# Decayed keys turned by DMA transposes from the second 512 tokens on, and the first early x tiles requested behind the output projection

## The chip, the cores and the metric

The kernel runs on the 8 cores of one Trainium2 chip. Each core takes two of the 16 sequences and works alone; no core sends data to another. The metric is the device time of the slowest core, in microseconds (us). Three executions of the kernel before gave a median of 3469.9 us (3467.58 to 3722.14).

## What is computed

One layer, on x of 16 sequences x 2048 tokens x 2048 features:

```
x = x + 0.5 * ffn(layernorm(x))
x = x + attn(layernorm(x))
x = x + 0.5 * ffn(layernorm(x))
```

ffn rounds its input row by row to 8-bit integers and its weight to -1, 0 or 1, multiplies them (2048 x 2048) and scales back. attn is gated linear attention with 16 heads of 128 features: q, k, v and a gate g (log-sigmoid) are projections of x; per head a 128x128 state follows S = S * exp(g) + k v^T and y = q S, token by token. The y of all heads is normalised and multiplied by the output weight Wo.

## The kernel before

**Tiling.** A core has 4096 tokens, in 8 slabs (g = 0 to 7) of 512 tokens; a slab is 4 tiles (t) of 128 tokens. TensorE goes through phases, each over one slab: P1 is the first ffn, H is the gate, key and query projections of 16 heads with the attention behind them, V is the values, P4 the output projection, P5 the second ffn (P6 is a last piece of it). The order is V(0), then for each g: H(g), P1(g+1), P4(g), V(g+1), P5(g). The phases P1, V, P4 and P5 consist of 16 groups (k) of 16 matmuls of 512 columns, written by `fat` (L511). A head of H has three groups of 16 matmuls (L597).

**Weights.** They pass through a ring of three SBUF buffers, one *unit* at a time: a head's 1.5 MB or a quarter of a 2 MB-unit matrix. The list `units` fixes the order. In slab 0 (and for heads 3, 7, 11 and 15 in slab 1) POOL reads the fp32 weight by a casting DMA (L446), and SP then writes the bf16 result to a scratch tensor in HBM (L412); afterwards SP reads from that scratch (L409). A load of unit n waits until TensorE is through with unit n - 3.

**A head.** ACT and DVE make decay factors from the gate. DVE writes the scaled keys kt, then the decayed keys kd (L795, two buffers, kd[h % 2]), then the scaled queries. `post(g, h)` runs on TensorE after the second projection group of head h + 1: four transposes of kd into PSUM (L546), then eight small matmuls for the scores (L554, L556). ACT copies the transposed keys to SBUF, into kdT (L1032). `step(g, hg, t)` runs after all three groups of a head, from head 4 on, and uses four heads' kdT (L571) and scores (L581, L584); a group of four heads is first used one head after its last one, and the last group in P1(g+1).

**SP's program.** SP works down one list: for each unit n it loads (or writes to scratch) unit n, and then runs what belongs to unit n - 3, called `done`: stores of the output, or the *crossings* (L370). A crossing is a DMA transpose of one normalised token tile nb, 128 x 2048 of 2 bytes, into the operand xT. Crossings for A (the next slab's P1) come behind heads 6 to 9. Everything on SP is in order: an instruction that waits holds back all behind it.

**Early x.** For g of 2 and more POOL asks for slab g's four x tiles ahead of time, cast to bf16, into qp and kdT (L463), once step(g - 2, 3, 3) is done; the buffers are idle then. DVE reads them in `ahead(g)`, behind quantise("C", g - 2) and before its first evacuation of P5(g - 2): 4 moments, a maximum and a minimum per tile. The same x is later loaded again into its residual buffer (L425), behind P5(g - 2).

Of the kernel before, what the change touches and what calls it, by code (L numbers as in the profile page):

```python
# [17 lines left out]
H = 16  # L18
SEQ = 2
L = 2048  # L20
TPS = 4
# [29 lines left out]
def emit(SEQ, L, known):  # L51
# [108 lines left out]
    with contextlib.ExitStack() as ctx:  # L160
# [27 lines left out]
        kdT = sb("kdT", 8 * 512, BF16, 2)  # L188
# [78 lines left out]

        XT = [count(f"turned{t}") for t in range(TPS)]

        def xTof(g):  # L270
            return xT[(g + 1) % 2]

# [47 lines left out]
        def crossed(kind, g):  # L320

            return (kind in "AL" and g >= 2) or (kind == "C" and g < NSL - 1)


        nb_sets = [("A", 0), ("L", 0)]
        for g in range(NSL):
# [28 lines left out]
        def _(e):  # L355
# [11 lines left out]
            def cross(kind, g, t):  # L367
# [3 lines left out]
                                      [:, :, t * 128:(t + 1) * 128], in_=nbt(t)  # L371
                                      ).then_inc(*XT[t].up(kind, g, by=16))

            def crossings(done):

                (kind, g), b = done
                if kind == "H" and crossed("A", g + 1) and 6 <= b <= 9 and g + 1 < NSL:
                    cross("A", g + 1, b - 6)
                if kind == "P1" and crossed("L", g) and b == 3:
                    cross("L", g, 0)  # L380
                if kind == "P4" and crossed("L", g + 1) and g + 1 < NSL and b == 0:
                    cross("L", g + 1, 1)
                if kind == "P4" and crossed("L", g + 1) and g + 1 < NSL and b == 1:
                    cross("L", g + 1, 2)
                    cross("L", g + 1, 3)
                if kind == "P4" and crossed("C", g) and b == 3:
                    cross("C", g, 0)
                if kind == "V" and g > 0 and b == 0:
                    cross("C", g - 1, 1)
                if kind == "V" and g > 0 and b == 1:  # L390
                    cross("C", g - 1, 2)
                    cross("C", g - 1, 3)

            for n in range(NU + 3):
                done = units[n - 3] if n >= 3 else (("none", 0), 0)
                if done[0][0] in ("P5", "P6"):
                    for t in range(3):
                        store(done, t)
                if n < NU:
                    (kind, g), b = units[n]  # L400
                    cols = NB * (384 if kind == "H" else 512)
                    scratch = PLAIN[kind][1] if kind in PLAIN else s_f
                    if not is_cast(n) and not is_kept(n):
                        before, kept = ring_before(n), kept_at(n)
                        e.wait_ge(*TD.of("unit", before))
                        if is_kept(before):
                            e.wait_ge(*WB[place(before)].of(before))
                        e.wait_ge(*WB[place(kept)].of(kept))
                        e.dma_start(out=buf(n)[:, 0:cols], in_=scratch[b]).then_inc(*RL[place(n)].up(n, by=16))  # L409
                    elif is_kept(n):  # L410
                        e.wait_ge(*(VD.of("tern", n, 3) if kind == "P1" else RC[place(n)].of(n)))
                        e.dma_start(out=scratch[b], in_=buf(n)[:, 0:cols]).then_inc(*WB[place(n)].up(n, by=16))  # L412
                if done[0][0] in ("P5", "P6"):
                    store(done, 3)
                else:
                    crossings(done)
# [5 lines left out]
        def _(e):  # L422
# [36 lines left out]
            for g in range(2, NSL + 1):  # L459
                if g < NSL:  # L460
                    e.wait_ge(*TD.of("Y", g - 2, 3, 3))
                    for t in range(TPS):
                        e.dma_start(out=xe(t), in_=xrows[g * TPS + t]).then_inc(*XE[t].up(g, by=16))  # L463
                    e.wait_ge(*VD.of("ev", ("P5", g - 2), 15))
                    load_x(g)
# [7 lines left out]
        def _(e):  # L473
            ti = 0
# [65 lines left out]

            def post(g, h):
                nonlocal ti
                e.wait_ge(*VD.of("kd", g, h))
                e.wait_ge(*SD.of("pT", ti - 2))
                for t in range(TPS):
                    tr = e.transpose(pT[ti % 2][:, t * 128:(t + 1) * 128],  # L546
                                     kd[h % 2][:, t * 128:(t + 1) * 128], ident[:])
                tr.then_inc(*TD.up("kdT", g, h))
                ti += 1
                e.wait_ge(*VD.of("qo", g, h))  # L550
                if g or h:
                    e.wait_ge(*(VD.of("Asb", g, h - 1) if h else VD.of("Asb", g - 1, H - 1)))
# [8 lines left out]
            def step(g, hg, t):  # L561
                now = S[(g * TPS + t) % 2]
                if t == 0:
                    e.wait_ge(*SD.of("kdT", g, 4 * hg + 3))
                    e.wait_ge(*VD.of("Asb", g, 4 * hg + 3))
                before = step_before(g, hg, t)
                if before is not None:
# [88 lines left out]
        def _(e):  # L656
# [132 lines left out]
            def decayed_keys(g, h):  # L789
                k2 = kt[h % 2][:].rearrange("p (t a c) -> p t a c", a=4, c=64)[:, :, 0:4:3, :]  # L790
                e.wait_ge(*SD.of("smx", g, h))
                e.wait_ge(*VD.of("ev", ("H", g), 3 * h + 1))
                f8 = smx[:, h * 20 + 4:h * 20 + 12].rearrange("p (t a) -> p t a", a=2) \
                    .unsqueeze(3).broadcast_to([128, TPS, 2, 64])
                e.tensor_tensor(kd[h % 2][:].rearrange("p (t a c) -> p t a c", a=2, c=64), k2, f8, ALU.mult  # L795
# [203 lines left out]
        def _(e):  # L999
# [41 lines left out]
            def heads(g):  # L1041
                for h in range(H):
# [13 lines left out]
                        e.wait_ge(*VD.of("cleared"))  # L1056
                    if g == 0 and h == 11:
                        e.wait_ge(*WB[3].of(aside[0]))
                    if h > 0:
                        keys_turned(g, h - 1)  # L1060
                    if h >= 4:
                        y_out(g, h // 4 - 1, h % 4)
# [4 lines left out]
                            turned("A", g + 1, i)  # L1067

            def tail(g, k):
                if k == 1:  # L1070
                    keys_turned(g, H - 1)
                if 2 <= k <= 5:
                    y_out(g, 3, k - 2)
# [125 lines left out]
```

## Time and profile before

| | |
|---|---|
| median of 3 executions | 3469.9 us |
| profiled execution, device time | 3467.16 us |
| its span, first to last instruction of core 7, the slowest | 3465.6 us |
| spans of cores 0 to 7 | 3457.2, 3444.7, 3453.1, 3458.6, 3454.9, 3440.9, 3464.2, 3465.6 us |
| mean granted TensorE clock of the cores | 0.990 to 0.992 |
| TensorE matmuls (PE) | 3321.8 us busy, 96% of the span |
| DVE, ACT | 2018.9 us (58%), 744.6 us (21%) |
| DMA queue of SP, of POOL | 49.3% and 14.6% of the 16 DMA engines' span |

A timeline row gives start, duration (us), engine, line, operation, tiles written and read, shapes and count; idle time before it and what ended that stand in brackets. Matmuls overlap, so what one costs is the distance between starts. SPq is SP's sequencer while it issues a DMA; the duration there is how long SP was held. "DMA to landing" is the time from issue to completion. A row of `stretches` gives the stretch, its length, the busy time and number of instructions of PE, PEld (weight loads), DVE, ACT and POOL, and then the granted TensorE clock, the share of DMA time and GB/s. All rows are of core 7 where no other is named.

### The profile page before, as it was taken

What the parts mean: (1) busy time and instruction counts of PE and PEld (TensorE: products, weight loads), DVE (VectorE), ACT (ScalarE), POOL (GpSimd) and SP (SyncE); (2) the same over time, 40 slices, a digit from 0 to 9 for tenths busy, and PEclk for the clock granted to TensorE, in tenths of its full rate; (3) what the DMA queues carried; (4) which work ended last, traced back from release to release, by engine and by line L of the source; (5) the groups of instructions that cost most, each with busy time, mean ns of one, the idle gap of its engine ahead of it and who ended that gap; (6) DMA issues with size and microseconds to landing.
All of it is one profiled execution on the core that took longest, in us unless ns stands there. A gap on an engine that the chain in (4) does not pass through costs nothing.

```text
span 3465.6 us, 49427 instructions; the slowest of 8 cores (3440.9 to 3465.6 us)
## 1 busy us (share of the span) xinstructions
PE 3321.8 (96%) x18210; PEld 1611.7 (47%) x18210; DVE 2018.9 (58%) x3783; ACT 744.6 (21%) x1297; POOL 48.3 (1%) x94
## 2 busy tenths in 40 slices
PE   1789998999999999999999999999999999999999
PEld 0334453445544454445544455444554455444544
DVE  5626767156672666637664476826667366635663
ACT  5312321023200221113211232002320032112210
POOL 0000000000000000000000000000000000000000
PEclk9899999999999999999999999999999999999999
DMA  7899979787566546665466655666556654553453
GB/s 221 193 225 204 219 179 231 202 199 195 177 194 200 170 159 183 191 198 170 150 188 204 177 169 171 182 200 172 176 168 197 202 157 161 163 170 145 153 176 134
DMA packets 227642, 634.68 MB, mean 183 GB/s; under 512 B 165856, under 2 KB 165888, under 8 KB 189520
## 3 DMA queue, kind: packets, MB, share of 16 engines
q1 hardware_dynamic: 215104, 553.68, 49.3%
q0 software_dynamic: 12304, 77.85, 14.6%
q8 instruction: 151, 2.47, 0.3%
q14 instruction: 83, 0.68, 0.1%
HBM read 585.35 MB, written 83.89 MB: 193 GB/s over the span
## 4 chain that ended last, share of the span: by engine, by line
PE 87%; DMA 9%; DVE 1%; issue 1%; another core or an unknown queue 1%; SPq 0%; ACT 0%; DVEq 0%; POOLq 0%; ACTq 0%; POOL 0%
PE pj L511 47%; PE pj L597 35%; DMA ring<-wh 2%; DMA s_v<-first 1%; DMA ring<-wv 1%; DMA s_h<-ring 1%; DMA fw<-fw 1%; PE pT L488 1%; DMA ring<-wo 1%; PE pP L571 1%; PE pY L581 1%; PE pT L546 1%; PE pA L554 1%; PE pY L584 1%
## 5 line engine op out<-in xcount | busy, mean ns | idle before, releaser
L511 PE MATMUL pj<-ring,xT 128*128 128x512 bf16 x8000 | 1755.4, 380 | 31.5 <-DVE bnA L722 12.4
L597 PE MATMUL pj<-xT,ring 128*128 128x512 bf16 x6144 | 1369.3, 380 | 28.2 <-DMA ring<-wh 23.6
L511 PEld LDWEIGHTS pj<-ring,xT 128*128 128x128 f16 (+1 forms) x8000 | 779.1, 98 | 955.0 <-issue 45.1
L597 PEld LDWEIGHTS pj<-xT,ring 128*128 128x128 bf16 x6144 | 590.4, 98 | 711.5 <-issue 40.8
L765 DVE TENSOR_TENSOR_SCAN Cs<-rest_s,lsg 128x512 f32<-128x512 bf16 x128 | 156.6, 1223 | 301.8 <-ACT lsg L1049 300.6
L962 DVE SCALAR_TENSOR_TENSOR ost<-pj,coC,res 128x512 f32<-128x512 f32 x112 | 84.1, 751 | 405.5 <-PE pj L511 405.5
L1046 ACT ACTIVATE lsg<-pj 128x512 f32<-128x512 f32 x128 | 76.4, 597 | 736.4 <-PE pj L597 729.6
L759 DVE SCALAR_TENSOR_TENSOR res<-pj,coA,res 128x512 bf16<-128x512 f32 x128 | 95.7, 748 | 174.4 <-PE pj L511 174.4
L804 DVE TENSOR_TENSOR qt<-pj,E 128x512 bf16<-128x512 f32 x128 | 88.4, 691 | 133.1 <-PE pj L597 133.1
L1039 ACT CAST vy<-pY 128x512 bf16<-128x512 f32 x128 | 75.0, 586 | 369.5 <-PE pY L584 349.4
L1083 ACT CAST vy<-pj 128x512 bf16<-128x512 f32 x128 | 74.9, 585 | 366.9 <-PE pj L511 366.9
L1051 ACT ACTIVATE E<-Dl 128x512 bf16<-128x512 f32 x128 | 80.6, 630 | 301.0 <-DVE sm L774 293.5
L833 DVE SCALAR_TENSOR_TENSOR S<-S,smx,pP 128x128 bf16<-128x128 bf16 x480 | 134.6, 342 | 12.8 <-DVE qp L812 0.5
L759 DVE SCALAR_TENSOR_TENSOR res<-pj,res 128x512 bf16<-128x512 f32 x128 | 88.2, 689 | 89.8 <-PE pj L511 89.8
L785 DVE TENSOR_TENSOR kt<-pj,E 128x512 bf16<-128x512 f32 x128 | 88.5, 692 | 77.3 <-ACT smx L1053 76.7
L1023 ACT ACTIVATE xT<-pT,bet,gam 128x512 bf16<-128x512 bf16 x128 | 92.2, 775 | 161.4 <-PE pT L488 161.4
L771 DVE TENSOR_TENSOR Dl<-Cs 128x512 f32<-128x512 f32 x128 | 88.6, 692 | 13.7 <-DVE Cs L765 0.5
L812 DVE TENSOR_TENSOR qp<-qt,smx 128x512 bf16<-128x512 bf16 x128 | 88.6, 692 | 13.7 <-DVE qt L808 0.5
L722 DVE BATCH_NORM_STATS2 bnC<-res 128x6 f32<-128x512 bf16 x128 | 88.8, 694 | 13.2
L1049 ACT ACTIVATE lsg<-lsg,one 128x512 f32<-128x512 f32 x128 | 92.5, 723 | 12.2 <-ACT lsg L1046 0.4
L722 DVE BATCH_NORM_STATS2 bnL<-res 128x6 f32<-128x512 bf16 x128 | 88.1, 689 | 9.2 <-DVE res L759 0.5
L1005 ACT ACTIVATE lnvC<-mvC,eps 128x4 f32<-128x4 f32 x8 | 2.4, 298 | 403.2 <-DVE mn4C L672 403.2
(121 smaller groups left out, 2187.1 us busy)
## 6 DMA issues: line engine op xcount, KB each, us to landing
ring<-s_h SPq DMA_DIRECT2D x108, 1536.0 KB, 8.2
ring<-s_f SPq DMA_DIRECT2D x60, 2048.0 KB, 9.3
ring<-s_v SPq DMA_DIRECT2D x28, 2048.0 KB, 9.9
ring<-s_o SPq DMA_DIRECT2D x28, 2048.0 KB, 9.8
out<-ost SPq DMA_DIRECT2D x128, 256.0 KB, 4.3
ring<-wh POOLq DMA_DIRECT2D x20, 1536.0 KB, 21.7
s_h<-ring SPq DMA_DIRECT2D x16, 1536.0 KB, 20.2
fw<-fw SPq DMA_DIRECT2D x16, 1024.0 KB, 35.9
```

Source lines behind the costliest of these rows:

```text
L511: return e.matmul(bank(phase, k)[:], xt[:, ic * SLAB + t * 128:ic * SLAB + (t + 1) * 128], buf(n)[:, ic * 512:(ic + 1) * 512], start=ic == ...
L597: mm = e.matmul(bank(phase, 3 * h + j)[:], buf(n)[:, ic * 384 + j * 128:ic * 384 + (j + 1) * 128], xt[:, ic * SLAB:(ic + 1) * SLAB], start ...
L722: e.bn_stats(bn[kind][:, (t * 4 + b) * 6:(t * 4 + b + 1) * 6], src[:, b * 512:(b + 1) * 512]).then_inc(*VD.up())
L759: e.scalar_tensor_tensor(x, bank(phase, k)[:], combo(t), x, ALU.mult, ALU.add).then_inc(*VD.up("ev", phase, k))
L765: e.tensor_tensor_scan(Cs[:], rest[:], lsg[:], 0.0, ALU.mult, ALU.add).then_inc(*VD.up())
L771: e.tensor_tensor(Dl[:].rearrange("p (n c) -> p n c", c=64), c64, c64[:, :, 31:32].broadcast_to([128, 8, 64]), ALU.subtract).then_inc(*VD. ...
L785: e.tensor_tensor(k2, p[:].rearrange("p (t a c) -> p t a c", a=2, c=64), E2[:].rearrange("p (t a c) -> p t a c", a=2, c=64), ALU.mult).the ...
L804: e.tensor_tensor(q3[:, :, 0:3:2, :], p[:].rearrange("p (t a c) -> p t a c", a=2, c=64), E1[:].rearrange("p (t a c) -> p t a c", a=2, c=64 ...
L812: e.tensor_tensor(qp[:, (h % 8) * 512:(h % 8 + 1) * 512].rearrange("p (t c) -> p t c", c=128), q192[:, :, 0:128], smx[:, h * 20:h * 20 + 4 ...
L833: e.scalar_tensor_tensor(nxt[:, hs], now[:, hs], smx[:, h * 20 + 16 + t:h * 20 + 17 + t], pP[:, i * 128:(i + 1) * 128], ALU.mult, ALU.add) ...
L1023: e.activation(dst[:, ic * 512:(ic + 1) * 512], pT[ti % 2][:, j * 512:(j + 1) * 512], ACTF.Identity, bias=bet[:, ic:ic + 1], scale=gam[:, ...
L1049: e.activation(lsg[:], lsg[:], ACTF.Ln, bias=one1[:]).then_inc(*SD.up("l", g, h))
```

## The change

Two things. From slab 1 on (`keys_crossed(g)`, g > 0), the four TensorE transposes of a head and ACT's copy are gone, and SP issues a DMA transpose of kd[h % 2] (128 x 512, 2 bytes) straight into kdT. It stands ahead of the load of the unit in turn. `step` waits for the two DMA counters in place of ACT's, and DVE's kd of head h waits for the crossing of head h - 2. And POOL waits, for g == 2 alone, until the last group of P4(0) before it asks for the early x tiles.

```
+        KX = [count(f"keys_turned{i}") for i in range(2)]
...
+        def keys_crossed(g):
+            return g > 0
...
+            def cross_keys(g, h):
+                e.wait_ge(*VD.of("kd", g, h))
+                e.wait_ge(*(TD.of("kv", g, h // 4 - 2, 3) if h >= 8 else TD.of("kv", g - 1, h // 4 + 2, 3)))
+                e.dma_start_transpose(out=kdT[:, (h % 8) * 512:(h % 8 + 1) * 512].rearrange("p (t c) -> p t c", c=128),
+                                      in_=kd[h % 2][:]).then_inc(*KX[h % 2].up(g, h, by=16))
...
                 if done[0][0] in ("P5", "P6"):
                     for t in range(3):
                         store(done, t)
+                if done[0][0] == "H" and keys_crossed(done[0][1]):
+                    cross_keys(done[0][1], done[1])
                 if n < NU:
...
                 if g < NSL:
                     e.wait_ge(*TD.of("Y", g - 2, 3, 3))
+                    if g == 2:
+                        e.wait_ge(*TD.of("fat", ("P4", 0), 15))
                     for t in range(TPS):
                         e.dma_start(out=xe(t), in_=xrows[g * TPS + t]).then_inc(*XE[t].up(g, by=16))
...
             def post(g, h):
...
-                e.wait_ge(*VD.of("kd", g, h))
-                e.wait_ge(*SD.of("pT", ti - 2))
-                for t in range(TPS):
-                    tr = e.transpose(pT[ti % 2][:, t * 128:(t + 1) * 128],
-                                     kd[h % 2][:, t * 128:(t + 1) * 128], ident[:])
-                tr.then_inc(*TD.up("kdT", g, h))
-                ti += 1
+                if not keys_crossed(g):
+                    e.wait_ge(*VD.of("kd", g, h))
+                    e.wait_ge(*SD.of("pT", ti - 2))
+                    for t in range(TPS):
+                        tr = e.transpose(pT[ti % 2][:, t * 128:(t + 1) * 128],
+                                         kd[h % 2][:, t * 128:(t + 1) * 128], ident[:])
+                    tr.then_inc(*TD.up("kdT", g, h))
+                    ti += 1
...
             def step(g, hg, t):
                 if t == 0:
-                    e.wait_ge(*SD.of("kdT", g, 4 * hg + 3))
+                    if keys_crossed(g):
+                        e.wait_ge(*KX[0].of(g, 4 * hg + 2))
+                        e.wait_ge(*KX[1].of(g, 4 * hg + 3))
+                    else:
+                        e.wait_ge(*SD.of("kdT", g, 4 * hg + 3))
...
             def decayed_keys(g, h):
+                if keys_crossed(g) and h >= 2:
+                    e.wait_ge(*KX[h % 2].of(g, h - 2))
...
-                    if h > 0:
+                    if h > 0 and not keys_crossed(g):
                         keys_turned(g, h - 1)
...
-                if k == 1:
+                if k == 1 and not keys_crossed(g):
                     keys_turned(g, H - 1)
```

## Rows read from the trace of the kernel before

**Rows 1.** The page: chain of waits, shares of the span by engine.

```profile
PE 87%; DMA 9%; DVE 1%; issue 1%; another core or an unknown queue 1%; SPq 0%; ACT 0%; DVEq 0%; POOLq 0%; ACTq 0%; POOL 0%
```

**Rows 2.** PE's waits, 400 to 700 us, then 700 us on: total, times, longest.

```profile
PE pj L511 <- DVE bnA L722: 12.4, 1, 12.4
PE pj L511 <- DMA ring<-wo: 1.7, 1, 1.7
...
PE pj L597 <- DMA ring<-s_h: 2.9, 1, 2.9
```

**Rows 3.** Timeline of PE, one head of slab 2.

```profile
1154.86 0.39 PE L546 MATMUL pT<-ident_s,kd 128*128 128x128 bf16 x4
1155.08 0.22 PE L554 MATMUL pA<-qt,kt 128*128 128x128 bf16 x1
...
1166.45 0.39 PE L546 MATMUL pT<-ident_s,kd 128*128 128x128 bf16 x4
```

**Rows 4.** Slab 0: landing of the first two wo casts, the last, then two s_v loads.

```profile
DMA to landing us min/median/max: 14.3/18.3/22.4
...
DMA to landing us min/median/max: 31.0/31.0/31.0
...
DMA to landing us min/median/max: 26.7/29.7/32.8
```

**Rows 5.** Timelines of PE and SP, slab 0's end: V(1) starts; its first loads.

```profile
576.37 112.38 PE L511 MATMUL pj<-ring,xT 128*128 128x512 bf16 x512 [12.43 <-DVE bnA L722]
...
549.32 16.86 SPq L409 DMA_DIRECT2D ring<-s_v  x3
```

**Rows 6.** Stretches: end of slab 0, then the heads of slab 2.

```profile
517.00:549.00 32.00, 30.41 (x177) 15.12 (x175) 22.34 (x35) 6.07 (x6) 2.64 (x5) 1.00 1.00 223
564.00:577.00 13.00, 0.63 (x2) 0.28 (x3) 11.68 (x31) 0.50 (x2) 0.00 (x0) 0.59 1.00 254
577.00:600.00 23.00, 23.00 (x101) 10.12 (x100) 23.00 (x21) 3.52 (x6) 0.00 (x0) 0.94 0.91 260
1105.00:1290.00 185.00, 185.00 (x1106) 92.91 (x1105) 120.47 (x259) 55.36 (x107) 2.12 (x4) 1.00 0.56 169
```

**Rows 7.** Early x tiles 3 and 4, issued at 519 us, then at 1313 us.

```profile
DMA to landing us min/median/max: 54.7/59.3/63.8
...
DMA to landing us min/median/max: 20.6/21.5/22.4
```

**Rows 8.** Timeline of DVE: first and last pass over early x, first P5 evacuation.

```profile
575.51 2.46 DVE L722 BATCH_NORM_STATS2 bnA<-qp 128x6 f32<-128x512 bf16 x4
...
600.36 2.27 DVE L740 TENSOR_REDUCE mnbA<-kdT 128x4 f32<-128x2048 bf16 x1
637.07 0.75 DVE L962 SCALAR_TENSOR_TENSOR ost<-pj,coC,res 128x512 f32<-128x512 f32 x1 [34.44 <-PE pj L511]
```

**Rows 9.** Line 370, all crossings: duration in ns, landing; then one issued alone.

```profile
L370 SPq DMA_TRANSPOSE xT<-nb x76: 1747/7822/15689, 573.9 to 3080.0; - x76
DMA to landing us min/median/max: 4.3/10.2/17.8
...
L370 SPq DMA_TRANSPOSE xT<-nb x1: 1747/1747/1747, 3054.0 to 3054.0; - x1
```

**Rows 10.** Timelines, slab 2: DVE's kd of one head; SP at the end of its projections.

```profile
1180.54 0.69 DVE L795 TENSOR_TENSOR kd<-kt,smx 128x512 bf16<-128x512 bf16 x1
...
1182.70 0.32 SPq L409 DMA_DIRECT2D ring<-s_h  x1
1183.14 7.80 SPq L370 DMA_TRANSPOSE xT<-nb  x1
```

**Rows 11.** Timeline of SP, slab 1: the scratch write of head 3.

```profile
722.03 0.33 SPq L412 DMA_DIRECT2D s_h<-ring  x1
```

**Rows 12.** Line 412: the landing of that write.

```profile
DMA to landing us min/median/max: 7.7/7.7/7.7
```

**Rows 13.** Timeline of PE, core 3: the start of V(1).

```profile
570.17 1.44 PE L511 MATMUL pj<-ring,xT 128*128 128x512 bf16 x3 [7.00 <-DMA ring<-s_v]
```

## The prediction

> **What bounds the kernel.** I read four views. The chain of waits comes first: 87% of it is TensorE and 9% DMA [rows 1]. So time taken out of TensorE's own stream counts one for one, nearly everywhere, and the DMAs count only where TensorE stands. The list of PE's waits says where that is: from 400 to 700 us two waits belong together, 1.7 us for the last wo cast and 12.4 us before V(1), and after 700 us the largest single wait is 2.9 us for a weight load [rows 2]. The 12.4 us are put down to DVE's pass over early x, but that pass starts at 575.51 us [rows 8] and gives V(1) nothing it needs. What ends then is a load: V(1)'s first unit was asked for at 549.32 us [rows 5], the two loads of that moment took 26.7 and 32.8 us to land [rows 4], and 549.3 + 26.7 = 576.0 us, just before V(1) starts at 576.37 us [rows 5]. The stretches give the reason: the DMA share is 1.00 from 517 to 549 us and from 564 to 577 us [rows 6]. In the heads of slab 2 TensorE is busy for all of 185 us at a DMA share of 0.56 [rows 6]. There it is TensorE alone that sets the pace.
>
> **Part 1, the transposes leave TensorE.** In a head the first transpose starts at 1154.86 us and the first score matmul behind the four at 1155.08 us: 0.22 us, with no wait between [rows 3]. The change takes this from 16 heads in each of 7 slabs, 112 in all: 112 x 0.22 = **24.6 us**. Rounding in the row leaves 23.5 to 25.8 us. ACT loses 112 copies, which I cost at nothing since ACT is not on the path; the scores and the mask on DVE come as before.
>
> **What comes for it: SP and the DMA queue.** The crossing of a head is a quarter of those that the kernel has. The trace has no crossing of this size, so I bound it. Of 76 large ones, the shortest hold of SP is 1.75 us and the shortest landing 4.3 us; that hold belongs to one issued with nothing ahead of it [rows 9]. The median is 7.8 us and 10.2 us [rows 9], for crossings issued 0.44 us behind a weight load, as in [rows 10]. So a key crossing holds SP between 0.44 us (a quarter of 1.75) and 7.8 us, and lands within 2 to 10 us. I take about 1 us and 4 us in an ordinary head, since it is issued into an empty queue: kd is complete at 1180.54 + 0.69 = 1181.23 us, and SP only asks for the next unit at 1182.70 us, when the head's projections are over [rows 10]. SP therefore sees kd 1.5 us before it would have been released anyway, and the load behind it moves by nothing or by tenths. The key DMA finds the previous load landed, a period of 11.59 us (1166.45 - 1154.86, [rows 3]) being longer than its flight. Who waits for it: `step` needs head 4hg + 3 one whole head later, 11.4 us against a landing of 4; DVE's kd of head h needs the crossing of h - 2, two heads later, 22 us. Behind head 15, two groups of P1 and a score block lie between. Cost on the path: 0.
>
> In heads 6 to 9 of a slab SP also issues a crossing for A, 7.8 us of hold [rows 10]. A period then holds 1 + 0.3 + 7.8 us and two gaps of 0.4, about 10 of the 11.4 us that a head takes after the change. It fits, with little left over.
>
> **Where it does cost: slab 1.** Heads 3, 7, 11 and 15 are still cast there, and SP is stuck until the cast has landed. It writes head 3 to scratch at 722.03 us [rows 11], and then today asks at once for head 4, for which TensorE already waits 2.9 us [rows 2]. Now head 1's key crossing goes between, behind a write that takes 7.7 us to land [rows 12]. Head 4's load is late by at least 0.4 us (the hold) and at most by the 7.7 us in which the write drains. I take **+2 us**: the engines are never idle meanwhile, so the queue only has the crossing's own data more to move. Heads 7, 11 and 15 have the same order, but their next load isn't waited for today.
>
> **Part 2, early x goes later.** The four tiles are asked for at 518 to 520 us, among the last cast, two scratch writes and V(1)'s loads. The first wo casts landed in 14.3 and 22.4 us, the last, issued just ahead of the x tiles, in 31.0 [rows 4]. SP can't ask for V(1) until it has landed. With x out of the way it should land in about 23 us, V(1)'s load goes out 8 us sooner, and has less beside it. The last two x tiles took 54.7 and 63.8 us, so nearly all four tiles moved before 576 us [rows 7]. Their work in a less loaded place is bounded by the 20.6 to 22.4 us that the same tiles need in slab 1 [rows 7], with a load beside them; I put it at 13 us of all engines. A saturated queue gives that back as it is. The two waits are 14.1 us [rows 2]; and the granted clock is 0.59 (of 2.4 GHz, so partly at 1.2) in the idle stretch and still 0.94 in the 23 us behind it [rows 6], so ending the stall returns up to 23 x 0.06 = 1.4 us more. I take **13 us**, between 0 and 15.5.
>
> The x tiles now start at 562.3 us, when P4(0) ends. DVE's pass takes 27.1 us (575.51 to 600.36 + 2.27, [rows 8]), 6.8 a tile, and must be over when the first group of P5(0) is, 60.7 us after V(1)'s start [rows 5, 8], so at about 623 us. The last tile has to land by 616 us, 54 us after the request. I expect 25 to 40 us: the DMA share from 577 to 600 us was 0.91 with the old x tiles in it [rows 6]. Cost 0.
>
> **Sum.** 3467.16 - 24.6 - 13 + 2 = **3431.6 us** against the profiled execution. The median of three is 2.7 us above that execution, so a median should lie between 3431.6 and 3434.3: I say 3433, which is -1.1%. Core 3, with a span of 3458.6 us and a wait of 7.0 us in place of 12.4 [rows 13], comes out at 3458.6 - 24.6 - 7 + 2 = 3429, so core 7 or 6 stays last.
>
> **Rivals.**
> - *x moved for nothing.* The queue was full before x was asked for (the second cast took 22.4 us [rows 4]), and scratch writes keep it full. V(1) still starts late: 3467 - 24.6 + 2 = 3445. Against it: core 3's wait is only 7.0 us [rows 13], so the load is near its need. 12%.
> - *x too late.* If the last tile takes 63.8 us again [rows 7], it lands at 626, DVE ends at 633 and P5(0) stands 10 us: 3442. The queue is emptier there. 6%.
> - *Small crossings disturb the loads.* 112 x 512 packets more, and a load or two late at each slab's start, where SP's queue also holds stores: 1.5 to 3 us a slab, 3442 to 3453. The share of 0.56 speaks against it. 8%.
> - *SP saturated: slower.* The place is heads 7 to 10 of slabs 1 to 6, where key crossing, load and crossing for A share SP. If a key crossing holds SP 7.8 us like a large one, a head takes 7.8 + 0.3 + 7.8 + 0.8 = 16.7 us of SP's 11.4; the lag is 5.3 a head, 21 us after four. Head 11's crossing starts that late and lands 10 us on, and the step behind head 12 stands about 21 + 10 - 12.5 = 18 us. Six slabs make 110 us: 3467 - 38 + 2 + 110 = 3541, slower by 2.1%. It decides from a hold of 2.5 us (lag begins), and is a net loss from about 4.6. For it: 7.8 is the median. Against: kd comes into an empty queue, where a crossing four times the size held 1.75 us. 6%, with half of it above 2%.
>
> The Trainium skill (VectorE: DVE Perf Modes, "The three transpose paths") prices a 128x128 bf16 transpose at 390 ns on TensorE and 1309 ns by the DMA crossbar, and its rules say to use TensorE where the result may go to PSUM. By its figures part 1 would return 448 x 0.39 = 175 us, where the rows show 0.055 us a transpose behind other work, and a key crossing would take 5.2 us, an estimate from that page that lies beyond the 4.6 of the last rival. The rule speaks against this change; the trace has 16 blocks landing in 4.3 us [rows 9], 0.27 each, and I follow the trace.
>
> **Chances and range.** The forecast (3426 to 3440) has 68%, the rivals 12, 6, 8 and 6. The range of 3423 to 3455 takes in all but the last, with the other bounds of the terms. 2% either way (69 us) is about what a measurement of this kernel can tell from no change. Faster by over 2% would need twice the gain: 2%. Slower by over 2%: 4%. Within 2%: 94%.
>
> **What would show it.** Right: a head's period of 11.37 us in place of 11.59; SP holds at keys of 1 us or so, landings under 5; V(1) starting by 565 us; head 4 of slab 1 waiting 3 to 6 us; early x landed by 602 us. Wrong: PE waiting at L571 for DMA, SP's loads sliding after head 10, DVE waiting before L795, or P5(0) waiting for a bank that DVE empties late.

## The result, and the profile after

| | before | changed |
|---|---|---|
| median of all executions | 3596.02 us (4) | 3433.89 us (4) |
| range | 3467.58 to 4092.39 | 3430.6 to 3650.42 |
| profiled execution | 3467.16 | 3432.75 |
| spans of the cores | 3440.9 to 3465.6 | 3415.1 to 3431.2 |

The ratio is 0.9889, with a 95% interval of 0.985 to 0.9927: about 1.1% faster, and clear of 1. It leaves out executions in which the cores of one half of the chip got a lower clock; two of the four before were such, which is why that median is so high. The point forecast was 3433.

The page of the changed kernel: its span and instruction count, the busy line, SP's DMA queue and the chain's shares.

```profile
span 3431.2 us, 48546 instructions; the slowest of 8 cores (3415.1 to 3431.2 us)
...
PE 3299.2 (96%) x17762; PEld 1588.8 (46%) x17762; DVE 2019.6 (59%) x3783; ACT 691.1 (20%) x1185; POOL 49.8 (1%) x94
...
q1 hardware_dynamic: 276032, 568.38, 53.5%
...
PE 89%; DMA 8%; DVE 1%; issue 1%; SPq 0%; ACT 0%; DVEq 0%; POOLq 0%; ACTq 0%; POOL 0%
```

TensorE has 448 matmuls fewer, ACT 112 copies fewer, and its share of the chain is 89%, where it was 87% [rows 1]: the bound has not moved. SP's queue is busier by 4 points of the DMA engines' time.

Line numbers have shifted: L546 is L565 and serves slab 0 alone, L554 is now L573, L597 is L620, L511 is L529, L409 is L424, L412 is L427, L370 is L376, L571 is L594, L795 is L820; the key crossing is L384.

**Part 1.** PE's timeline in slab 2, the first score matmul of two heads in a row, answers to [rows 3].

```profile
1152.45 0.22 PE L573 MATMUL pA<-qt,kt 128*128 128x128 bf16 x1
...
1163.82 0.22 PE L573 MATMUL pA<-qt,kt 128*128 128x128 bf16 x1
```

The distance is 11.37 us, where it was 11.59. The key crossing (L384) and the crossings of normalised tokens (L376), durations in ns and landings in us, answer to [rows 9]; SP's timeline around the end of a head answers to [rows 10].

```profile
L384 SPq DMA_TRANSPOSE kdT<-kd x112: 1172/1175/2713, 690.7 to 3245.8; - x112
...
DMA to landing us min/median/max: 2.4/2.4/21.9
```

```profile
L376 SPq DMA_TRANSPOSE xT<-nb x76: 1746/7750/11481, 580.5 to 3048.3; - x76
DMA to landing us min/median/max: 4.3/9.9/17.2
```

```profile
1167.34 1.18 SPq L384 DMA_TRANSPOSE kdT<-kd  x1
1168.67 0.46 SPq L424 DMA_DIRECT2D ring<-s_h  x1
1169.23 8.24 SPq L376 DMA_TRANSPOSE xT<-nb  x1
1178.50 1.17 SPq L384 DMA_TRANSPOSE kdT<-kd  x1
```

and DVE's kd of the second of these heads:

```profile
1177.68 0.68 DVE L820 TENSOR_TENSOR kd<-kt,smx 128x512 bf16<-128x512 bf16 x1
```

A key crossing holds SP 1.18 us and lands in 2.4 (median). Key crossing, load and crossing of x fill 10.1 us (1167.34 to 1169.23 + 8.24), and the next key crossing goes out 11.2 us after the first: SP is nearly full here, but it waits for the keys and not the keys for it. It is free at 1177.47 us, kd is complete at 1178.36, and the crossing goes out at 1178.50.

**Part 2.** The waits of PE from 400 to 700 us, then the longest from 700 us on, answer to [rows 2].

```profile
PE pj L620 <- DMA ring<-wh: 2.3, 1, 2.3
PE pP L594 <- DVE Asb L844: 2.0, 1, 2.0
...
PE pj L620 <- DMA ring<-s_h: 2.4, 1, 2.4
```

Both waits, for the last wo cast and before V(1), are gone. The landings of the last wo cast, of V(1)'s first two loads, and of early x tiles 3 and 4 answer to [rows 4, 7]; SP's first load of V(1) to [rows 5].

```profile
DMA to landing us min/median/max: 27.9/27.9/27.9
...
DMA to landing us min/median/max: 14.1/17.5/21.0
...
DMA to landing us min/median/max: 19.7/20.9/22.0
```

```profile
554.69 16.40 SPq L424 DMA_DIRECT2D ring<-s_v  x3
```

V(1)'s first load landed at 554.69 + 14.1 = 568.8 us. POOL asked for x at 571.1 us, once the last group of P4(0) was over, so the load had some 2 us to spare on this core. Between the request of the last wo cast and this landing lie 42.6 us (526.2 to 568.8), where they were 58.3 (517.7 to 576.0).

The stretches around it answer to [rows 6] (length, busy time and count of PE, PEld, DVE, ACT and POOL, granted clock, DMA share, GB/s):

```profile
526.00:554.00 28.00, 28.00 (x162) 13.91 (x160) 19.88 (x32) 5.06 (x5) 0.53 (x1) 1.00 0.99 234
554.00:571.00 17.00, 17.00 (x98) 8.46 (x97) 10.87 (x18) 3.04 (x3) 0.00 (x0) 1.00 0.95 309
571.00:594.00 23.00, 23.00 (x109) 10.43 (x107) 18.18 (x37) 3.91 (x8) 2.11 (x4) 1.00 1.02 238
594.00:631.00 37.00, 37.00 (x173) 16.78 (x172) 19.70 (x17) 5.86 (x10) 0.00 (x0) 1.00 0.93 256
1092.00:1271.00 179.00, 179.00 (x1034) 88.33 (x1033) 118.08 (x252) 47.87 (x92) 2.12 (x4) 1.00 0.69 183
```

The engines are no less full than before; the full stretch has moved behind the first load of V(1), where TensorE does not need them, and the granted clock is 1.00 in all of it. DVE's timeline shows the price (answers to [rows 8]): a wait of 3.5 us for x, and 16.5 us left over before P5(0) where it had 34.4.

```profile
585.82 2.47 DVE L745 BATCH_NORM_STATS2 bnA<-qp 128x6 f32<-128x512 bf16 x4 [3.54 <-DMA qp<-x]
...
629.42 0.75 DVE L987 SCALAR_TENSOR_TENSOR ost<-pj,coC,res 128x512 f32<-128x512 f32 x1 [16.48 <-PE pj L529]
```

**Where the time went, by stage.** I measured these from the starts of the first projection matmul of a slab's heads and of the first group of the phase behind them, on all eight cores of one profiled execution each. H is a slab's heads; F0 reaches from the end of slab 0's heads to the start of slab 1's. Mean of the cores, and their range:

```
                     H(0)                F0                  H(1)                H(2)     F1
before               216.4 (211-220)     243.2 (239.7-247.3) 184.6 (182.2-188.4) 182.3    227.8
changed              220.8 (215-227)     231.1 (231.0-231.2) 180.9 (179.2-183.2) 178.9    227.6
keys alone           218.4 (212-223)     243.4 (239.9-245.4) 180.2 (178.9-183.5) 178.9    227.6
later x alone        218.9 (213-223)     231.9 (231.0-234.7) 183.7 (182.5-185.9) 182.3    227.8
changed, again       219.0 (215-223)     231.7 (231.0-234.0) 182.0 (179.9-185.5) 178.9    227.6
keys not turned      218.0 (215-221)     231.1 (231.0-231.2) 179.4 (178.9-179.9) 178.9    227.6
x behind cast        214.8 (209-223)     232.3 (231.0-233.9) 184.8 (181.2-187.7) 179.4    227.8
later x, all slabs   215.3 (212-222)     231.1 (231.0-231.2) 180.4 (178.9-182.1) 179.3    227.6
```

(In the rows "x behind cast" and "later x, all slabs", pairs of cores took 0.7 to 1.8 us more in most of the slabs from 2 on; the mean granted clock of these cores was 0.986 to 0.991, of the others 0.990 to 0.993.) Each later slab gains 3.3 us in its heads and 0.2 in the phase behind them: 16 x 0.22.

### The profile page after: what moved, and what is told of

Its sections match the earlier page's. It is cut to its first block, busy times and chain, and to the rows that moved or that the text cites. A ratio compares the mean times of both kernels' runs of the same rounds, so it can differ in the third digit from the quotient of the medians.

```text
span 3431.2 us, 48546 instructions; the slowest of 8 cores (3415.1 to 3431.2 us)
## 1 busy us (share of the span) xinstructions
PE 3299.2 (96%) x17762; PEld 1588.8 (46%) x17762; DVE 2019.6 (59%) x3783; ACT 691.1 (20%) x1185; POOL 49.8 (1%) x94
## 4 chain that ended last, share of the span: by engine, by line
PE 89%; DMA 8%; DVE 1%; issue 1%; SPq 0%; ACT 0%; DVEq 0%; POOLq 0%; ACTq 0%; POOL 0%
PE pj L529 50%; PE pj L620 34%; DMA ring<-wh 4%; DMA ring<-wv 1%; DMA fw<-fw 1%; PE pT L506 1%; DMA s_h<-ring 1%; PE pP L594 1%; PE pY L604 1%; PE pA L573 1%; PE pY L607 1%; SPq L365 0%; DVE ring L774 0%; PE pA L575 0%; DMA ring<-s_h 0%
## 5 line engine op out<-in xcount | busy, mean ns | idle before, releaser
L529 PE MATMUL pj<-ring,xT 128*128 128x512 bf16 x8000 | 1753.0, 380 | 16.8 <-DVE ring L774 9.6
L620 PE MATMUL pj<-xT,ring 128*128 128x512 bf16 x6144 | 1372.6, 381 | 29.9 <-DMA ring<-wh 23.0
L529 PEld LDWEIGHTS pj<-ring,xT 128*128 128x128 f16 (+1 forms) x8000 | 778.8, 98 | 938.1 <-issue 26.7
L620 PEld LDWEIGHTS pj<-xT,ring 128*128 128x128 bf16 x6144 | 591.4, 98 | 715.5 <-issue 46.9
L745 DVE BATCH_NORM_STATS2 bnC<-res 128x6 f32<-128x512 bf16 x128 | 88.8, 694 | 13.9 <-DVE res L782 0.9
L820 DVE TENSOR_TENSOR kd<-kt,smx 128x512 bf16<-128x512 bf16 x128 | 87.7, 685 | 2.1 <-DMA kdT<-kd 1.3
```

Source lines behind the costliest of these rows:

```text
L529: return e.matmul(bank(phase, k)[:], xt[:, ic * SLAB + t * 128:ic * SLAB + (t + 1) * 128], buf(n)[:, ic * 512:(ic + 1) * 512], start=ic == ...
L620: mm = e.matmul(bank(phase, 3 * h + j)[:], buf(n)[:, ic * 384 + j * 128:ic * 384 + (j + 1) * 128], xt[:, ic * SLAB:(ic + 1) * SLAB], start ...
L745: e.bn_stats(bn[kind][:, (t * 4 + b) * 6:(t * 4 + b + 1) * 6], src[:, b * 512:(b + 1) * 512]).then_inc(*VD.up())
```

## The experiments

**Keys alone.** The changed kernel without the wait before the early x requests.

```
-                    if g == 2:
-                        e.wait_ge(*TD.of("fat", ("P4", 0), 15))
```

> The key crossings alone; early x is asked for where the kernel before asks. My theory, that the two parts are independent and add: 16 heads x 0.22 us in each of seven slabs, 24.6 us, so 3443 to 3446 us, a ratio near 0.9929; each later slab's stretch from its first head projection to P1 falls from 182.2 to 178.9 us; V(1) still stands 7 to 12 us. The rival, that most of the gain hangs on the x requests (a fuller queue makes the key crossings late while x is in flight), says 3455 us or more.

Measured: 3440.6 to 3445.59 us, median 3443.5, ratio 0.9927 (0.9908 to 0.9946). V(1) stands 11.0 us for its load on the slowest core, and the F0 column is that of before. The term of 24.6 us holds, and the rival (3455 us or more) falls. The wait, on core 0 of this kernel:

```profile
PE pj L526 <- DMA ring<-s_v: 11.0, 1, 11.0
```

**Later x alone.**

```
         def keys_crossed(g):
-            return g > 0
+            return False
```

> The later x requests alone; all keys are turned on TensorE. My theory: the stall before V(1) goes, so the stretch from P1(1) to the first head of slab 1 falls from 240 to 247 us to about 231.5 us on every core, and the slowest core gains 13 to 16 us if the heads of slab 0 take the same: 3453 to 3456 us, ratio 0.996. The rival, that what is saved there comes back as longer loads in slab 0's heads or in slab 1 (those heads were 7.2 us longer on core 7 in the one profile of the changed kernel, before any changed instruction), says 3462 us or more, with slab 0's heads at 222 us or more on most cores.

Measured: 3449.88 to 3453.95 us, median 3452.56, 0.9952 (0.9933 to 0.9971). F0 falls to 231 to 234.7 us. The rival asked for slab 0's heads at 222 us or more on most cores; one core has that (223.1), and their mean is 218.9: the time didn't come back. By the medians beside them (before 3466.6 in seven executions, changed 3429.9 in four), the parts are worth 23 and 14 us, and together 37.

**The changed kernel again.** No edit.

> The changed kernel once more, to see its spread and slab 0's heads in another execution. If the 4 us by which slab 0's heads were longer on the mean of the cores are chance, they lie near 216 to 219 us here on the mean, and the time is 3428 to 3434 us. If they belong to the change, they are again 220 us or more on the mean. Sum of the parts: the gain of this one equals those of the two single edits, 24.6 + 14, within 3 us.

Measured: 3425.94 to 3432.99 us, 0.9884 (0.9858 to 0.9911). Slab 0's heads come to 219.0 on the mean. That lies at the border of the two branches of the expectation. But the code of that stage is unchanged in all eight rows of the table, and its mean runs from 214.8 to 220.8. So the longer heads of slab 0 in the first profile of the changed kernel (220.8) are within the spread of this stage, in which TensorE waits for casts (23.0 us in six waits on core 7 of the changed kernel). The gain is that of the two parts.

**Keys not turned.** From slab 1 on, no transpose by either engine, and nothing waits for one, DVE's kd included. The kernel leaves the turned keys out, so its output isn't that of the layer; only its time is of use.

```
-                if done[0][0] == "H" and keys_crossed(done[0][1]):
-                    cross_keys(done[0][1], done[1])
...
-                    if keys_crossed(g):
-                        e.wait_ge(*KX[0].of(g, 4 * hg + 2))
-                        e.wait_ge(*KX[1].of(g, 4 * hg + 3))
-                    else:
+                    if not keys_crossed(g):
                         e.wait_ge(*SD.of("kdT", g, 4 * hg + 3))
```

> From slab 1 on the keys are not turned at all: neither by TensorE nor by DMA, and nothing waits for it, so the state update there uses old data. Everything else as in the changed kernel. This takes away all that the key crossings cost. My theory says that they cost nothing on the path from slab 2 on and at most 2 us in slab 1: 3429 to 3433 us, the changed kernel minus 0 to 2. The rival, that 57344 further packets slow the loads here and there, says 5 us or more below the changed kernel.

Measured: 3423.43 to 3424.38 us, against 3425.94 to 3432.99 beside it: 6 us by the medians, more than I expected (0 to 2). The place is as expected: from slab 2 on the stretches are equal to 0.1 us, and slab 1's heads fall from 182.0 (worst core 185.5) to 179.4 (worst 179.9). The other two profiled executions of the changed kernel have 180.9 (183.2) and 181.3 (184.5), so the crossings cost 1.5 to 2.6 us there on the mean of the cores and 3.3 to 5.6 between the worst ones, by one execution without them. The rival named the size, my theory the place. Core 4 of the changed kernel, again, and of this one, PE's waits in slab 1:

```profile
PE pj L620 <- DMA ring<-s_h: 3.0, 1, 3.0
PE pj L620 <- DMA ring<-wh: 1.6, 1, 1.6
```

```profile
PE pj L615 <- DMA ring<-s_h: 0.9, 1, 0.9
```

**Each key crossing seven times.** This tests the prediction's slower rival: six more crossings of kd into idle staging space, in slabs 1 to 6. The edit also has DVE wait for them before it writes kd again, and its output evacuations before they use the space.

```
...
+                    for d in dumps:
+                        e.dma_start_transpose(out=d.rearrange("p (t c) -> p t c", c=128),
+                                              in_=kd[h % 2][:]).then_inc(*KD.up(g, h, by=16))
```

> In slabs 1 to 6 SP issues each key crossing seven times, once into kdT and six times into a part of the output staging buffer that is idle then; kd is only rewritten when all seven have landed. One crossing holds SP 1.17 us, so seven hold it 8.2 us: this sets up the state of the prediction's slower rival, a hold of 7.8 us a head. My theory, that SP's hold counts only where it exceeds a head's 11.4 us: SP needs 8.2 + 0.5 + 8.2 us plus gaps in heads 7 to 10, lags 5 to 6 us a head, and by head 12 TensorE stands at the step or at a weight load for 10 to 20 us a slab: 60 to 120 us in six slabs, 3490 to 3550 us, with the stalls on the waits for the crossings or the loads in heads 11 to 13 and none before head 8. The opposing theory, that the queue's data is what counts: 7 x 57344 packets spread evenly, a few tenths of a us on every head from head 1 on, and under 30 us in all.

Measured: 3687.7 us, 1.0646 (1.0628 to 1.0664), 254 us above the changed kernel; I expected 60 to 120. The heads of slabs 2 to 6 take 207 to 211 us on the mean of the cores, some 30 more each, and those of slab 1 245 us (up to 262), some 64 more. SP's timeline, core 0, slab 2, one late head:

```profile
1279.59 1.19 SPq L386 DMA_TRANSPOSE kdT<-kd  x1
1280.87 9.05 SPq L395 DMA_TRANSPOSE ost<-kd  x6
1290.08 0.47 SPq L435 DMA_DIRECT2D ring<-s_h  x1
1290.64 6.46 SPq L378 DMA_TRANSPOSE xT<-nb  x1
```

and what TensorE waits for there:

```profile
1279.84 9.58 PE L631 MATMUL pj<-xT,ring 128*128 128x512 bf16 x32 [5.04 <-DMA ring<-s_h]
1297.45 8.75 PE L631 MATMUL pj<-xT,ring 128*128 128x512 bf16 x32 [3.56 <-DMA ring<-s_h]
1314.53 0.58 PE L605 MATMUL pP<-vy,kdT 128*128 128x128 bf16 x4 [4.54 <-DMA kdT<-kd]
```

The seven hold SP 10.2 us and not 8.2; that the later ones are held by the data queued ahead is my reading. So SP has no reserve even in heads 0 to 6, and waits of 0.4 to 1.8 us stand there too, before the stalls of 3.6 to 5.0 us. The mechanism of the rival exists, at the step's wait for the crossing and at the loads; a hold of 1.18 us is far from it. The price per slab (30 us, 64 in slab 1) is more than the rival's 18. The run can't part SP's hold from the data of six more crossings, which come with it.

**Key crossing behind the load.**

```
                 if done[0][0] in ("P5", "P6"):
                     for t in range(3):
                         store(done, t)
-                if done[0][0] == "H" and keys_crossed(done[0][1]):
-                    cross_keys(done[0][1], done[1])
...
+                if done[0][0] == "H" and keys_crossed(done[0][1]):
+                    cross_keys(done[0][1], done[1])
                 if done[0][0] in ("P5", "P6"):
                     store(done, 3)
```

> Each key crossing stands behind the load of the unit in turn in place of ahead of it (and ahead of the crossing for A). My theory of the two kinds of hold, that SP is held by the data queued ahead: the hold goes from 1.2 us to 5 us or more and the landing from 2.4 to 8 to 10 us. The step needs it within 11 us, so slabs 2 to 7 lose 0 to 3 us each, mostly at heads 8 and 12, and the load of head 4 in slab 1 leaves at once, which returns up to 2 us there: 3430 to 3450 us. The rival, that the hold is a matter of the crossing's own descriptors and not of what is ahead, says hold 1.2 us, landing up to 10 us, and the changed kernel's time within 2 us.

Measured: 3441.16 and 3436.14 us, too few for an interval. The mean granted clock in the profiled one was 0.985 to 0.990 on cores 4 to 7 and 0.991 to 0.993 on cores 0 to 3, so I read the latter. Core 0:

```profile
L384 SPq DMA_TRANSPOSE kdT<-kd x112: 1195/1710/3110, 695.1 to 3226.5; - x112
...
DMA to landing us min/median/max: 5.8/7.4/15.6
```

The hold is 1.7 us and not 5; the landing goes from 2.4 to 7.4 us. My theory of the hold fails for a crossing this small: a load ahead delays its landing and hardly holds SP. Slabs 2 to 7 take 178.2 to 178.9 us on these cores, as in the changed kernel, and slab 1's heads 179.8 to 180.6, so 7.4 us still fits in the 11.4 that the step leaves. Whether this order is as good as the changed kernel's, two executions don't tell.

**Slab 0 too.**

```
         def keys_crossed(g):
-            return g > 0
+            return True
```

> The keys are turned by DMA in slab 0 too. There SP stands at each scratch write until the cast has landed, so a head's crossing leaves two heads late. My theory: TensorE saves 16 x 0.22 = 3.5 us and loses it again at the four steps' first use, where the crossing of head 4hg + 3 waits behind the cast of head 4hg + 5; each of four steps stands 3 to 8 us, partly in place of the wait for the next cast: slab 0's heads at 222 to 240 us instead of 216 to 221 on the mean, 3432 to 3450 us. The rival, that casts bound slab 0 anyway so nothing changes, says heads of slab 0 at 216 to 221 us and 3428 to 3434 us.

Measured: 3510.07 to 3533.56 us, 1.0162 (1.0136 to 1.0187). Slab 0's heads take 287 us on the mean, some 68 more; I expected up to 20. The direction and the place were right. PE's waits in slab 0, core 0:

```profile
PE pP L594 <- DMA kdT<-kd: 89.9, 3, 35.5
PE pj L620 <- DMA ring<-wh: 8.9, 1, 8.9
```

Three steps stand 20 to 36 us each (20.4, 35.5 and 33.9). I had expected the crossing to leave late, behind a cast. That is the smaller part: those that the three steps wait for went out 0.1 to 6.3 us after DVE had written their kd and 2.0 to 6.2 us before TensorE stood, and took 22.2, 40.7 and 39.8 us to land. The second:

```profile
L384 SPq DMA_TRANSPOSE kdT<-kd x1: 3352/3352/3352, 362.0 to 362.0; - x1
...
DMA to landing us min/median/max: 40.7/40.7/40.7
```

Nor was the queue full all that time. After the third was asked for, at 444.9 us, the DMA share was 0.06 for 6 us. Under way were this crossing, a scratch write that took 36.1 us to land and a cast that took 30.7:

```profile
445.00:451.00 6.00, 6.00 (x35) 2.79 (x33) 5.51 (x12) 0.13 (x1) 0.00 (x0) 1.00 0.06 8
```

What held them is not shown. POOL's timeline has the other half: it asked for no cast for 41.8 us around the second step.

```profile
416.82 0.53 POOL L461 DMA_DIRECT2D ring<-wh  x1 [41.83 <-PE pP L594]
```

While TensorE stands at a step it finishes no head, and POOL doesn't ask for the next cast, since a cast waits for the unit three back. So each wait also empties the pipe of casts, which my estimate left out, as it did the landing.

**x behind the cast.** In slab 1 POOL asks for head 3's cast ahead of the four residual x tiles.

```
                     e.wait_ge(*VD.of("ev", ("P5", g - 2), 15))
+                    if g == 2:
+                        cast(unit_of[("H", 1), 3])
                     load_x(g)
...
-                        if late(h):
+                        if late(h) and h > 3:
```

> POOL asks for the cast of slab 1's head 3 first and for slab 2's four residual x tiles behind it, in place of the other way round; the rest as in the changed kernel. My theory: what is left of the waits in slab 1's heads (their stretch is 180 to 185 us against 178.9 in later slabs) is the cast of head 3 sharing the engines with 4 x tiles. The cast lands in 12 to 15 us instead of 20 to 22, and the stretch falls to 179 to 180 us on all cores: 1 to 4 us less than the changed kernel on its slowest core. The rival, that the wait comes from the key crossing put between the scratch write and head 4's load, says the stretch stays at 181 us or more on the mean.

Measured: 3433.69 to 3442.03 us, 0.9918 (0.9905 to 0.9931). The cast lands in 13.9 us (21.2 in the changed kernel), as expected, and the stretch grows: 181.2, 185.0, 184.4 and 186.8 us on cores 0 to 3 (the granted clock of the others was lower, 0.986 to 0.989). Head 4's load, core 3: 20.2 us to land against 9.4, and TensorE stands 4.8 us for it in place of 1.2. Core 3 of this kernel, then of the changed one, again:

```profile
719.18 1.44 PE L622 MATMUL pj<-xT,ring 128*128 128x512 bf16 x3 [4.77 <-DMA ring<-s_h]
```

```profile
712.73 1.02 PE L620 MATMUL pj<-xT,ring 128*128 128x512 bf16 x4 [1.20 <-DMA ring<-s_h]
```

The x tiles only changed their victim.

**x after head 2.** The same with x behind head 2 too: POOL asks for it once TensorE is through with that head's projections.

```
                     if g == 2:
                         cast(unit_of[("H", 1), 3])
+                        e.wait_ge(*TD.of("proj", 1, 2, 2))
                     load_x(g)
```

> In slab 1 POOL asks for the cast of head 3 first, then waits until TensorE is through with head 2, and only then asks for slab 2's four residual x tiles (needed by DVE from head 5 on). My theory after the last experiment, that the x tiles take the engines from whatever load is in flight, and that the loads of heads 3 and 4 are the only ones in slab 1 without slack: with x behind them the stretch of slab 1's heads falls to 179 to 180 us on all cores (changed kernel: 179 to 185), and the slowest core gains 1 to 4 us: ratio 0.987 to 0.988. The rival, that x is needed at once, says DVE waits for x at heads 5 to 8 and the stretch stays at 181 us or more.

Measured: 3441.02 to 3442.86 us, 0.9946 (0.993 to 0.9963): worse again, and by neither theory; DVE waits for no x. Core 0, where slab 1's heads take 196.8 us: the wait, and the landings of the key crossings of heads 3 and 4. (Core 2, with 196.4 us, stands 11.4 us for a cast instead.)

```profile
PE pP L597 <- DMA kdT<-kd: 16.2, 1, 16.2
```

```profile
L384 SPq DMA_TRANSPOSE kdT<-kd x2: 1191/1522/1852, 713.9 to 724.6; - x2
...
DMA to landing us min/median/max: 26.9/27.1/27.2
```

With x, two loads and, from 725.8 us on, a cast in flight together, a crossing that usually lands in 2.4 us took 27, and the first step stood 16.2 us for it. A full queue isn't all of it. In the middle of that wait:

```profile
730.00:738.00 8.00, 0.00 (x0) 0.00 (x0) 0.00 (x0) 0.00 (x0) 0.00 (x0) 0.50 0.26 48
```

For 8 us the DMA engines were 0.26 busy while both crossings, loads and the cast were still out, as in slab 0 of the run "Slab 0 too". The key crossings now have only 11.4 us to spare, whatever holds them.

**Later x in all slabs.**

```
-                    if g == 2:
-                        e.wait_ge(*TD.of("fat", ("P4", 0), 15))
+                    e.wait_ge(*TD.of("fat", ("P4", g - 2), 15))
```

> The wait for the last group of the output projection stands before the early x requests of every slab, not of slab 2's alone. My theory, that the wait pays only where V's first load is late, which is slab 0: every later stretch is as before (227.6 us from P1 to the next heads), and the time is the changed kernel's within 2 us. The rival, that later x holds back DVE's pass and with it P5, says 1 to 8 us a slab more.

Measured: 3425.06 to 3430.22 us, 0.9912 (0.9892 to 0.9932) on a chip where the kernel before took 3460.5. F1 stays at 227.6. As expected, as far as ratios of different chips can tell: no gain and no loss beyond their intervals.

**Crossings from head 4 of slab 1 on.**

```
-        def keys_crossed(g):
-            return g > 0
+        def keys_crossed(g, h):
+            return g > 1 or (g == 1 and h >= 4)
...
```

The callers pass the head along.

> The changed kernel, but in slab 1 heads 0 to 3 are turned by TensorE as before; DMA crossings begin at head 4 of slab 1. It costs TensorE 4 x 0.22 = 0.9 us and takes four crossings (and head 1's place between the scratch write and head 4's load) out of the stretch where casts, x tiles and loads share the engines. My theory, that the crossings cost time in slab 1 alone and there at head 4's load: the stretch of slab 1's heads is 180 to 181.5 us on every core, its worst core 2 to 4 us better than the changed kernel's (182 to 185.5), and the time 2 to 4 us below the changed kernel beside it. The rival, that the crossings' cost there sits at heads 7, 11 and 15 too, or that the worst core is chance, says the two are the same within 1.5 us.

> The changed kernel beside the last one, on the same chip, to compare with it: 0.987 to 0.991 of the kernel before, slab 1's heads 180 to 182 us on the mean of the cores and up to 185 on the worst.

Measured: 3426.5, 3430.93 and 3431.68 us (0.9896, 0.988 to 0.9911), beside 3429.04, 3431.79 and 3432.42 for the changed kernel (0.99, 0.9884 to 0.9915). The stretch of slab 1's heads is 179.8 to 180.3 us on cores 0, 1 and 4 to 7; on cores 2 and 3 the granted clock was lower in it (0.82 on core 2) and it took 218.1. The changed kernel has 179.5 to 180.8 on the same six cores, and its two worst, 183.4 and 184.5, are cores 2 and 3. So my theory is not shown: where the two can be compared they differ by 0.4 us on the mean. The time is the same within 1.5 us, as the rival said. Whether it is better by 1 us can't be told from these runs. No version tried beats the changed kernel clearly.

## Why the prediction came out as it did

- **The step that failed** is the one on what a measurement can tell: "2% either way (69 us) is about what a measurement of this kernel can tell from no change", with 94% put on that band. The change is 1.1%, and its interval of 0.985 to 0.9927, 0.4% to either side, excludes 1; four executions of the changed kernel lay within 7 us of each other (3425.94 to 3432.99). So the gain that the sum itself gave, 35 us, was one that the measurement resolves, and the prediction should have been of a gain and not of no change.
- **The terms that failed with it** are slab 1's (+2 us forecast, nothing measured against the kernel before) and the landing of the last cast in part 2 (23 us forecast, 27.9 measured). Both are taken up below.
- **The total** was 3433 forecast and 3433.89 measured; the mechanism of part 1 was right, and that of part 2 in the main. That it agrees to 1 us is partly luck. Core 7 was the slowest in both profiled executions. Its slab 0 heads took 7.1 us more, which no term has; F0 took 16.1 us less, where 13 was said and 15.5 was the bound; slab 1's heads took 5.2 us less, where some 3.3 - 2 = 1.3 was said. Of single cores the gain was 22.8 to 44.6 us. The medians of the executions side by side, 37 us, bear the sum out better than one core does.
- **Part 1, 24.6 us**: right, to the row. 3.5 us a slab; the edit alone gives 23 us of median. The distance between starts in one head priced 448 transposes.
- **The crossing's own cost in SP and in flight**: 1 and 4 us forecast, 1.18 and 2.4 measured. The Trainium skill (VectorE: DVE Perf Modes, "The three transpose paths") prices one 128x128 block at 1309 ns by DMA; that would make 4 x 1.31 = 5.2 us of the four blocks, an estimate. The trace measures 2.4 us to landing, and decides.
- **Slab 1, +2 us**: the place was right and the size was not. Against a kernel without any crossing they cost 1.5 to 2.6 us there on the mean and 3.3 to 5.6 between the worst cores. But the term was added to the kernel before, and against that nothing of it shows: core 7 waited 2.9 us for head 4's load before and 2.4 after, where 3 to 6 was said, and the mean of the cores in slab 1's heads, apart from the 3.3 us of part 1, moved by -0.4 to +0.8 us in three executions. The kernel before lost 2.4 us on the mean there (184.6 against 182.2) with its transposes on TensorE. Why it did is open.
- **Part 2, 13 us**: measured 14 in the edit alone, and 12 on the mean in F0. How it comes about was only half right. I expected the last cast in 23 us; it took 27.9. The gain came mostly from V(1)'s load, in 14.1 us instead of 26.7. Early x landed in 14.6 to 22.0 us, sooner than the 25 to 40 I allowed, at 594.7 us. V(1) started at 571 us and not by 565, since slab 0's heads were 7 us longer on this core.
- **The rivals.** "x moved for nothing" falls: 11 us of wait with the old requests, none with the new. "x too late" falls by 16.5 us of slack. "Small crossings disturb the loads" is true in slab 1 alone. (A key crossing is 544 packets by the queue's row of the page, 60928 more for 112, and not 512.) "SP saturated" is real as a mechanism and far from this kernel.

What stays open: why slab 0's heads spread over 6 to 14 us from core to core, and their mean over 6 us from execution to execution; and why crossings took 22 to 42 us in slab 0 and 27 in slab 1 when x came after head 2. All of these had a POOL cast beside them and loads or a scratch write, but the DMA engines were at 0.06 and 0.26 of their time in stretches of two of these flights, so that a full queue doesn't explain them.

## What to carry to other kernels

Where TensorE bounds the kernel, small work in its stream is worth the distance between starts times the count, and a DMA can take it over if a whole period lies between its issue and its use (here 11.4 us, against landings of 2.4 and, behind a load, 7.4). Before adding such a DMA, find where the engines are already full: in that place it cost 1.5 to 2.6 us on the mean and 3.3 to 5.6 on the worst core here, and 68 us on the mean where casts and scratch writes ran beside it all the time. Moving a bulk transfer out of a full stretch paid where what it landed beside had slack: four tiles moved behind the output projection gave 14 us. Four others, asked for 10 and 31 us later inside slab 1, cost about 6 and 12 us against the medians of the changed kernel (for the first on another chip) and of its version with later x in all slabs.

## What was not expected of the hardware

- The hold of the issuing engine depends on the size of the transpose and on what is queued. Alone, 512 KB held SP 1.75 us and 128 KB 1.17; behind a load of 1.5 MB, 7.8 and 1.7 us.
- The landing of a small crossing varies with what else is in flight: 2.4 us in the clear, 7.4 behind one load, 11 to 13 at the start of slabs 2 to 6 and 21.9 at that of slab 1, 27 with two loads, a cast and x out, 40.7 beside a scratch write and a cast. The Trainium skill (DMA: Bandwidth & Descriptors, "Issuing engines are not separate DMA queues") says that DMAs of different issuing engines run on the same 16 DMA engines and interleave. The trace agrees: x asked for by POOL behind the cast made SP's load of head 4 land in 20.2 us instead of 9.4. But sharing isn't the whole of the long landings, which held stretches of 6 and 8 us with the engines at 0.06 and 0.26.
- F0 took 231.0 to 231.2 us on all eight cores of the first profile of the changed kernel, from 239.7 to 247.3, once its one late load was in time; other profiles of it have one or two cores at 233 to 234.6. In this kernel a stage that differs from core to core has waits in it, and the stages from slab 2 on, which agree to 0.3 us, have TensorE full.
